# First destinations read out of the loaded edges, features loaded behind them, block limits set ahead of the gathers

## The reference

```
h = relu(layernorm(x))                       # block 0
norm = dinv[src] * dinv[dst]                 # dinv = 1/sqrt(degree), 0 without edges
m = norm * (h[dst] + (h[dst] * h[src]) @ W1.T + b1)
x = x + leaky_relu(segment_sum(m, dst))
h = relu(layernorm(x))                       # block 1, two mean convolutions
h = relu(h @ Ws0.T + mean(h[src] by dst) @ Wn0.T + c0)
x = x + h @ Ws1.T + mean(h[src] by dst) @ Wn1.T + c1
```

## Time and profile before

| | us |
|---|---|
| three runs, median (range) | 4112.94 (4110.04 to 4121.45) |
| the profiled execution: time / span | 4104.02 / 4102.3 |
| PE busy | 3648.9 (89%) |
| POOL busy | 2880.8 (70%) |
| DVE busy | 2018.2 (49%) |
| ACT busy | 1181.0 (29%) |
| chain that ended last | PE 46%, POOL 33%, issue 10%, DVE 6%, DMA 4% |

### The profile page before, as it was taken

How to read it: one execution, slowest core, us unless ns; L and a number is a source line. 1 busy time by engine, 2 the same in 40 slices (tenths; PEclk the granted TensorE clock), 3 DMA queues, 4 the chain that set the end, 5 groups by cost and what they waited for, 6 DMA issues and landing times.

```text
span 4102.3 us, 66912 instructions
## 1 busy us (share of the span) xinstructions
PE 3648.9 (89%) x24703; PEld 2328.6 (57%) x24703; DVE 2018.2 (49%) x5265; ACT 1181.0 (29%) x3014; POOL 2880.8 (70%) x2906
## 2 busy tenths in 40 slices
PE   0028989989999999998999999999999999999999
PEld 0025666656666666665556555555655666666565
DVE  3589988977778788872232322323221221311311
ACT  0043455556656666661020210202100000100100
POOL 5503677777777777754777777777757777777775
PEclk9999999999999999999999999999999999999999
DMA  5172465556656666667667577676787677677675
GB/s 158 45 180 81 139 204 193 190 191 207 209 193 224 219 214 213 224 234 243 249 222 267 207 288 256 225 251 238 267 280 260 245 254 283 221 277 263 233 274 204
DMA packets 385930, 905.09 MB, mean 221 GB/s; under 512 B 74847, under 2 KB 319528, under 8 KB 365378
## 3 DMA queue, kind: packets, MB, share of 16 engines
q1 hardware_dynamic: 193377, 590.39, 38.9%
q0 software_dynamic: 134256, 278.85, 22.6%
q10 hardware_dynamic: 57968, 31.48, 2.8%
HBM read 662.42 MB, written 238.96 MB: 220 GB/s over the span
## 4 chain that ended last, share of the span: by engine, by line
PE 46%; POOL 33%; issue 10%; DVE 6%; DMA 4%; ACT 0%; POOLq 0%; ACTq 0%; DVEq 0%; SPq 0%
PE ps L1455 35%; POOL arena L1253 30%; PE ps L1368 6%; PE ps L1426 3%; DMA arena<-parts,arena 3%; POOL arena L1218 2%; DVE arena L1680 2%; DVE arena L1683 2%; PE ps L1403 1%; DMA arena<-in_dst 1%; POOL arena L1243 0%; DVE arena L1698 0%; DVE arena L1696 0%; DVE arena L1697 0%; DMA table<-arena 0%
## 5 line engine op out<-in xcount | busy, mean ns | idle before, releaser
L1253 POOL DMA_INDIRECT arena<-parts,arena x2690 | 2714.7, 1009 | 927.5 <-issue 811.8
L1455 PE MATMUL ps<-arena 128*128 128x384 bf16 (+1 forms) x15778 | 3032.4, 328 | 17.1 <-DVEq L1757 13.5
L1455 PEld LDWEIGHTS ps<-arena 128*128 128x128 bf16 x15778 | 1527.2, 98 | 923.8 <-issue 28.0
L1049 ACT ACTIVATE arena<-ps 128x392 bf16<-128x392 f32 x1824 | 902.3, 497 | 1335.9 <-PE ps L1426 1317.5
L1426 PE MATMUL ps<-arena 128*128 128x196 bf16 (+1 forms) x5102 | 1036.6, 239 | 98.7 <-DVE arena L1683 91.1
L1708 DVE TENSOR_TENSOR arena<-arena 128x640 bf16<-128x640 bf16 (+1 forms) x587 | 265.8, 463 | 1237.6 <-PE ps L1368 1226.3
L1426 PEld LDWEIGHTS ps<-arena 128*128 128x128 bf16 x5102 | 481.0, 101 | 316.6 <-DVE arena L1683 95.9
L1368 PE MATMUL ps<-arena 128*128 128x384 bf16 (+1 forms) x2690 | 544.8, 331 | 107.2 <-DMA arena<-parts,arena 107.1
L1680 DVE TENSOR_TENSOR arena<-arena 128x768 bf16<-128x768 bf16 (+3 forms) x881 | 474.1, 538 | 242.6 <-PE ps L1426 236.7
L1683 DVE TENSOR_TENSOR arena<-arena 128x1176 bf16<-128x1176 bf16 (+4 forms) x881 | 554.5, 629 | 0.0
L1368 PEld LDWEIGHTS ps<-arena 128*128 128x128 bf16 x2690 | 258.3, 98 | 280.2 <-issue 129.3
(11 more groups left out here) (155 smaller groups left out, 1179.4 us busy)
## 6 DMA issues: line engine op xcount, KB each, us to landing
arena<-counts SPq DMA_DIRECT2D x100, 3136.0 KB
counts<-arena SPq DMA_DIRECT2D x54, 3136.0 KB
arena<-parts,arena POOLq DMA_INDIRECT x2690
arena<-parts SPq DMA_DIRECT2D x28, 672.0 KB, 9.7
arena<-table SPq DMA_DIRECT2D x196, 64.0 KB
parts<-arena ACTq DMA_DIRECT2D x110, 96.0 KB
parts<-arena SPq DMA_DIRECT2D x14, 679.0 KB, 7.0
parts<-arena SPq DMA_DIRECT2D x86, 96.0 KB
```

What stands on the lines that cost most here:

```text
L1049: act.activation(stage[k][:, :, a - g * P:b - g * P], ps[:, unit_bank(q), 0:(b - a) * tiles].rearrange("p (n a) -> p a n", n=b - a), ACT.C ...
L1253: pool.indirect_dma_start(ring[:, m % RSUBS * CHUNKS + c, 0:W0 if nth == 0 else W1C], None, parts_of[nth], bass.IndirectOffsetOnAxis(ap=ta ...
L1455: m = pe.matmul(bank(b, 0, w), stage[k][:, a, :], Xp[:, a, 0:w], start=e == 0, stop=e == tiles - 1, skip_group_check=True)
```

## The change

- The load of single words, its tile `first_i` and its semaphore `s_first` are gone. DVE waits for `s_dst` at 48 instead and reads the first destinations from `dst_i` with a step of 128 words; its later wait for `s_dst` is gone, too.
- ACT waits for `s_dst` at 48 before it issues the loads of `x`.
- POOL sets `room` and `tail_room` before its wait for `near_i`, and so ahead of the gathers, instead of after gather 20.

```diff
         @block.sync
         def _(sp):
-            with nc.allow_non_contiguous_dma(reason="single words and runs of five"):
-                sp.dma_start(first_i[0:iters, :], dst.rearrange("(i k e) -> i k e", k=SLOTS, e=P)[:, :, 0]).then_inc(s_first, 16)
+            with nc.allow_non_contiguous_dma(reason="single words"):
                 sp.dma_start(dst_i[0:iters - 1, :], bass.AP(dst.tensor, 0, [[STEP, iters - 1], [1, STEP + 1]])).then_inc(s_dst, 16)
...
         def _(act):
+            act.wait_ge(s_dst, 3 * 16)
             for i in range(loops):
...
             pool.memset(eps_c[:, :], EPS).then_inc(s_const, 1)
 
+            done = 0
+            for k, (a, n, vs) in enumerate(batches):
+                pool.memset(room[:, k:k + 1], float(P * vs[0])).then_inc(s_room, 1)
...
             pool.wait_ge(s_prepared_dve, 3)
             for t in range(tiles):
...
                                         bass.IndirectOffsetOnAxis(ap=near_i[:, t:t + 1], axis=0)).then_inc(s_neargot[q % 7], 16)
-                if t == 20:
-                    done = 0
-                    for k, (a, n, vs) in enumerate(batches):
...
-            dve.wait_ge(s_first, 16)
+            dve.wait_ge(s_dst, 3 * 16)
             dve.wait_ge(s_iden, 1)
-            dve.tensor_scalar(first_li[0:iters, :], first_i[0:iters, :], P - 1, None, ALU.bitwise_and)
-            own(dve.tensor_scalar(first_hi[0:iters, :], first_i[0:iters, :], 7, None, ALU.arith_shift_right))
+            firsts = dst_i[:, 0:STEP].rearrange("i (k e) -> i k e", e=P)[:, :, 0]
+            dve.tensor_scalar(first_li[0:iters, :], firsts, P - 1, None, ALU.bitwise_and)
+            own(dve.tensor_scalar(first_hi[0:iters, :], firsts, 7, None, ALU.arith_shift_right))
...
             dve.wait_ge(s_const, 4)
-            dve.wait_ge(s_dst, 3 * 16)
             own(dve.tensor_tensor(down, dst_i[:, 0:STEP], dst_i[:, 1:STEP + 1], ALU.subtract))
```

More of the change, by code:

```diff
@@ L374, in program @@
         pad_t = part(2 * pad // P)
-        first_i, first_li, first_hi = (part(SLOTS, dt=I32) for _ in range(3))
+        first_li, first_hi = (part(SLOTS, dt=I32) for _ in range(2))
         zero = part(deepest_tail)
@@ L404, in program @@
         s_const = sem("s_const")
-        s_first = sem("s_first")
         s_dst = sem("s_dst")
@@ L1211, in _ @@
             pool.memset(eps_c[:, :], EPS).then_inc(s_const, 1)
+            done = 0
+            for k, (a, n, vs) in enumerate(batches):
+                pool.memset(room[:, k:k + 1], float(P * vs[0])).then_inc(s_room, 1)
+                done += 1
+                for i in range(1, len(vs)):
+                    if vs[i] != vs[i - 1]:
+                        pool.wait_ge(s_room, done)
+                        pool.affine_select(out=room[:, k:k + 1], in_=room[:, k:k + 1], compare_op=ALU.is_gt, fill=float(P * vs[i]),
+                                           base=i, pattern=[[0, 1]], channel_multiplier=-1).then_inc(s_room, 1)
+                        done += 1
+            pool.memset(tail_room, float(P * tail_visits[0])).then_inc(s_room, 1)
+            done += 1
+            for i in range(1, tails):
+                if tail_visits[i] != tail_visits[i - 1]:
+                    pool.wait_ge(s_room, done)
+                    pool.affine_select(out=tail_room, in_=tail_room, compare_op=ALU.is_gt, fill=float(P * tail_visits[i]),
+                                       base=i, pattern=[[0, 1]], channel_multiplier=-1).then_inc(s_room, 1)
+                    done += 1
             pool.wait_ge(s_prepared_dve, 3)
```

## The result

The changed kernel took 4102.2 us (median of 20 runs, 4094.1 to 4114.4), the kernel before 4114.0 (20 runs, 4104.8 to 4121.5). The ratio is 0.9974, with a 95% interval of 0.9967 to 0.9981: 10.7 us faster, 7.8 to 13.6 (the two medians alone are 11.8 apart). The forecast was -7.5 us, 4105.4. By its own mark of 0.3% this isn't yet "faster", though it is clear of no change. The profiled execution of the changed kernel has a span of 4106.9 us, longer than the one shown of before (4102.3); single executions lie up to 20 us apart, so the two spans settle nothing. What can be compared to a tenth of a us is the head.

A forecast was written before the change was run, and what follows sets the result against it. TensorE and its feed bound the kernel from about 203 us, behind a serial, unhidden head. Gathers -10.2 and start +2.7 gave -7.5 us, applied to the median 4112.9: 4105.4 us, range 4093 to 4117 for 8 in 10.

The forecast's parts named there:

- mark of 0.3%: Whole kernel: a measurement tells about 0.3%, 12 us, from no change; faster by more than that was given 0.20.
- The body follows the head one to one: TensorE's stage from about 203 us on: a head ending some us earlier brings all of it forward by as much.
- The block leaves the file of gathers: POOL's setting of room and tail_room no longer interrupts the gathers: -16.3 us; in its new place it ends near 21.
- The gathers pay for L1568 to L1570: Gathers now meet the three DVE instructions that caught POOL's selects: 6.1 us given back, bounds 0 and 7.6.
- Rival 2: Gathers don't stop under the three DVE instructions that make the records: -13.6 us, 4099.3; chance 0.11.
- L1565 costs 2.6 before and after: DVE's check that dst is sorted catches one gather, losing 2.6 us in both kernels, so no net change.
- dst_i at 28.0: Start of the head: DVE waits for the dst_i load until 28.0 instead of 25.28, +2.7 us; bounds 18.3 and 30.8.
- Rival 1: Start of the head: dst_i alone loads at full rate, DVE starts at 18.3; -17.2 us, 4095.7; chance 0.14.
- x lands near 95 and costs nothing: x, held behind dst_i, lands near 95, before the 121 at which loss begins: no cost, 26 us in hand.
- split of the 143 us: POOL's stretch of gathers, 37.66 to 180.9: 98 gathers at 1.25 make 122.5 us, the rest foreign.
- Rival 3: x lands near 145, past the 121 of first loss, so DVE's counts end behind the gathers: +16.5 us, 4129.4; chance 0.05.
- -10.2 was forecast for the file of gathers: Net on POOL's gathers in the head: -16.3 us removed plus 6.1 us given back makes -10.2 us.

The follow-up runs named there:

- e1: The kernel before with only the setting of room and tail_room moved ahead of the gathers: ratio 0.9979, 8.6 us faster.
- e2: The changed kernel with the setting of room and tail_room put back behind gather 20: ratio to the kernel before 1.0003.
- e3: The changed kernel with the loads of x issued at once, not held for dst_i: ratio to the kernel before 0.9995.
- e4: The changed kernel with the dst_i load cut into 112 and 12 rows instead of 124: ratio to the kernel before 0.9951, 20.2 us faster.
- e9: The changed kernel with dst_i cut into 112 and 12 rows and the limits, except their first memset, behind the last gather: ratio to before 0.995, 20.6 us faster.
- e10: e9 with the load of src and the store of records also cut into 112 and 13 rows: ratio to the kernel before 0.9943, 23.5 us faster.
- e8: The changed kernel without the two DVE instructions that check that dst is sorted; one execution, first gather 1.29 us, DVE start at 30.25.
- e11: The kernel before, unchanged, run again for its trace on the chip of e9 and e10: records issued at 203.74 us.
- e5: The changed kernel with dst_i loaded as 124 rows without the odd last word, that word loaded separately; one execution, about 0.81 us a row.

## Why the prediction was right

| | head: records issued, us against before | ratio, as us (interval) |
|---|---|---|
| the change | -7.8 | -10.7 (-13.6 to -7.8) |
| e1 | -10.1 | -8.6 (-12.8 to -4.9) |
| e2 | -1.1 | +1.2 (-2.5 to +4.9) |
| e3 | -2.9 | -2.1 (-5.8 to +1.2) |
| e4 | -20.1 | -20.2 (-25.1 to -15.2) |
| e9 | -21.8 | -20.6 (-25.9 to -14.8) |
| e10 | -25.9 | -23.5 (-29.2 to -18.1) |

- **The body follows the head one to one.** Right: in all seven the head's shift lies in the interval of the time (for the change at its edge). The intervals are 3 to 6 us wide on each side, so this is shown to that much and no better; e4, e9 and e10, with 20 us and more, carry it. The 2.9 us by which the change did better than its head aren't repeated by any other version, and no trace shows them. They lie inside the spread of the measurement, at its edge; that they are nothing else isn't shown. In the head the forecast is -7.5 against -7.8; in the time it lies just short of the interval (-7.8 to -13.6), so it is the head that it had right to a few tenths.
- **The block leaves the file of gathers** (-16.3). Right: no select stands behind the first gather, and 16.3 us are gone. The block took 7.2 us in its new place instead of the 9 reckoned, and ended at 19.9 instead of 21.
- **The gathers pay for L1568 to L1570** (6.1 forecast). Measured: 1.29 + 2.28 + 2.15 = 5.7, and the same within 0.1 in e1, e2, e3, e4, e9 and e10. Rival 2 is out. The Trainium skill (SBUF — State Buffer, "Who interferes with whom") reports a tensor_tensor that didn't stall such a DMA, and says beside it that a DVE instruction with two inputs in SBUF contends with a GpSimd instruction that reads SBUF. The prediction took up only the first. Here a gather, which takes its indices from SBUF, takes 4.25 us under a TENSOR_TENSOR and 1.29 without it (e8), which goes with the second; the measurement decides.
- **L1565 costs 2.6 before and after.** Off by 0.7: it caught the first gather 0.4 us after its own start instead of 0.8, and 3.3 were lost.
- **dst_i at 28.0** (+2.7). Measured 25.99, +0.7. The forecast named 27 to 29 as its sign, and 26 to 31 as the bounds outside which it would be wrong: 25.99 misses the first and lies on the edge of the second. The mis-sized term is the load: from its first row to the end of its last it took 23.6 us, where 25.2 and 0.3 to 0.5 were reckoned. Whether the forecast was too long isn't settled by that, for with the same load and x held e2 has 26.17 and e8 30.25, so 28.0 lies inside what the load does from one chip or execution to another, and the +0.7 isn't clear either: the kernel before starts at 25.28, at 25.90 in e11. Rival 1, with 18.3, is out all the same, and e5 shows that the odd last word isn't the cause of the slow rate. (Its 18.3 adds up to 18.0 to 18.2 from the forecast's own terms, which changes nothing.) That the hold of x earns anything wasn't priced, since I compared the start with the old one only; e3 puts it at about 4 us.
- **x lands near 95 and costs nothing.** It landed at 93.88, by the forecast's own steps. The first half of the sentence held; the second didn't quite: with x there, DVE takes six counts in a row, and these catch gathers for 3.9 us where before it was 1.9. This term was missing, and the forecast's own split of the 143 us showed it: 122.5, 16.3 and 2.6 leave nearly 2 us over, most of it the gathers caught under counts. e10 shows it from the other side: x 27.6 us earlier is worth 3.2. The chain of waits of the changed kernel even runs through x:

```profile
1.53 24.44 DMA arena<-in_dst
...
55.40 38.38 DMA arena<-in_x
93.88 1.47 DVE stats L1584 x7
```

  It does so because a caught gather ends with the instruction that caught it; POOL had its next gather ready all along, and the loss is 0.6 us for each, not the 27.9 us that DVE waited for x. Rival 3, with its point at 121, stayed 27 us away. (The first row of the chain starts at 1.53, where L857 is issued, the load of the last word; it is one word behind the 124 rows of L855 on the same queue, and the rows are what takes the time.)

The sum: -10.2 was forecast for the file of gathers and -8.3 measured (+0.7 for L1565, -0.4 for the three, +1.9 for the counts, -0.3 for the 1.29 us of the first gather, which is now part of its 4.25), and +2.7 for the start, measured +0.7. The two errors, +1.9 and -2.0, cancel, which is luck: the -7.5 is better than its terms.

## What to carry to other kernels

Work moved off a serial file of an engine frees its own time only; what it was itself waiting for is passed on to the next instruction of that engine, here 5.7 of 16.3 us. A load's number of rows can matter more than its bytes: 124 rows went at 0.7 to 0.8 us a row, on four engines by all that was measured, and with 112 + 12 rows the same bytes were there by 11.1, hardly behind the tile that DVE needs from POOL anyway. And a span that nothing hides, before the long stage begins, comes back one to one, as far as intervals of 3 to 6 us tell; but each part has to be tried by itself: of these three edits one carried the gain, and against it alone (e1) the other two cost the head 0.6 us at its start and 1.7 in caught gathers, in one trace each: -10.1 with the first alone, -7.8 with all three.

## What the runs showed of the hardware

- A gather that starts under L1565, L1569 or L1570, VectorE instructions with two inputs in SBUF, isn't slowed but held: it ended 0.8 to 1.2 us behind the other's end (L1565: 41.46, gather: 42.63; L1569: 50.37 and 51.19; L1570: 53.78 and 54.60). It holds for the plain L1568 (one input, 1.83 us) as well: it ended at 46.85 and the gather at 47.67. So two inputs aren't what it takes. It doesn't hold for the reduce L1566, beside which a gather took 0.94.
- A gather is held by one such instruction only: under L1568 to L1570, 8.8 us in a row (45.02 to 53.78), POOL issued three, and each got through at the seam.
- dst_i goes at 16 to 18 GB/s on each of four engines (12804 bytes in 0.72 us in the change); as 125 rows, at 0.54 us a row, it was there 12 us sooner, on the same chip (28.08 and 16.34). That these are four and five engines with 31 and 25 rows each is in line with the shares of the queue, and no view shows the single engines.
- On one chip (granted clock 0.94, the kernel before at 4969 us) VectorE stood up to 9.2 us at a time between instructions, in stretches from 85 to 185 us, in all four kernels that were traced there. What it waited for stays open; the trace names only "issue" and "remote". Whether it belongs to the chip or to those executions isn't shown.
